# Splitting the last expert tiles, moving the weight maximum, filling idle TensorE time and finer loads ahead of the combination

## What is computed

```
h = layernorm(x) * (1 + ca) + sa
x = x + ga * linear_attention(h)      # 16 heads of 8, running sums over the tokens
h = layernorm(x) * (1 + cb) + sb
h = rmsnorm(h @ W_in.T, in_norm_w)    # then a router picks 2 of 8 experts per token
out = sum over the two: gate_e * rmsnorm((silu(h @ Wg[e].T) * (h @ Wu[e].T)) @ Wd[e].T, enorm_w[e])
x = x + gb * (rmsnorm(out, out_norm_w) @ W_out.T)
```

## Time and profile before

| | |
|---|---|
| median of the timed runs | 414.87 us |
| time of the profiled execution | 414.08 us |
| its span, first to last instruction | 412.2 us |
| PE busy | 354.4 us (86%) |
| DVE busy | 323.8 us (79%) |
| ACT busy | 291.9 us (71%) |
| POOL busy | 236.5 us (57%) |
| mean granted TensorE clock | 0.939 |

### The profile page before, as it was taken

How to read it: one execution, slowest core, us unless ns; L and a number is a source line. 1 busy time by engine, 2 the same in 40 slices (tenths; PEclk the granted TensorE clock), 3 DMA queues, 4 the chain that set the end, 5 groups by cost and what they waited for, 6 DMA issues and landing times.

```text
span 412.2 us, 12923 instructions
## 1 busy us (share of the span) xinstructions
PE 354.4 (86%) x3757; PEld 307.9 (75%) x3758; DVE 323.8 (79%) x1037; ACT 291.9 (71%) x814; POOL 236.5 (57%) x211
## 2 busy tenths in 40 slices
PE   7899998999999999982069999999999999990464
PEld 4788886888888888861049889989899898980443
DVE  5568998899999999976928887878778877870696
ACT  5465776888888888546328878778778787773595
POOL 0665585688888888856341645454454445453441
PEclk9999998999999999995559999999999999997698
DMA  7899000000000000111423333333333333213833
GB/s 217 356 368 363 2 28 26 8 30 27 26 26 26 26 26 26 34 40 51 131 40 54 68 71 70 62 71 60 64 64 71 60 69 65 57 34 110 351 94 94
DMA packets 46563, 35.68 MB, mean 87 GB/s; under 512 B 36291, under 2 KB 42070, under 8 KB 45750
## 3 DMA queue, kind: packets, MB, share of 16 engines
q1 hardware_dynamic: 41862, 25.40, 21.9%
q0 software_dynamic: 4544, 9.39, 7.0%
q10 hardware_dynamic: 128, 0.53, 0.5%
HBM read 18.69 MB, written 13.47 MB: 78 GB/s over the span
## 4 chain that ended last, share of the span: by engine, by line
PE 70%; DVE 10%; ACT 6%; issue 5%; DMA 4%; POOL 1%; SPq 1%; DVEq 0%; ACTq 0%; POOLq 0%
PE bank L1474 12%; PE bank L1723 9%; PE bank L1724 8%; PE bank L1725 8%; PE bank L1738 4%; PE bank L1740 4%; PE bank L1554 4%; PE bank L1739 4%; PE bank L1497 3%; DVE prod L960 2%; ACT junk L835 2%; DVE wmaxs L1056 1%; PE bank L1561 1%; DMA cst<-consts 1%; PE bank L1581 1%
## 5 line engine op out<-in xcount | busy, mean ns | idle before, releaser
L559 POOL DMA_INDIRECT expert_rows<-late,to_place x78 | 79.2, 1015 | 85.9 <-DVE late L1333 73.3
L1723 PE MATMUL bank<-late,w_hi 128*128 128x256 f16 x312 | 86.4, 277 | 15.1 <-DMA late<-dispatched 13.7
L1724 PE MATMUL bank<-late,w_hi 128*128 128x256 f16 x312 | 86.4, 277 | 0.0
L1725 PE MATMUL bank<-late,w_lo 128*128 128x256 f16 x312 | 86.3, 276 | 0.0
L518 POOL TENSOR_TENSOR kv<-kv,v 128x1024 f32<-128x1024 f32 x32 | 67.7, 2134 | 32.0 <-ACT kv L686 32.0
L1319 DVE SCALAR_TENSOR_TENSOR kv<-bank,uscale,kv 128x512 f32<-128x512 f32 x78 | 58.5, 750 | 30.4 <-ACT kv L777 18.6
L536 POOL DMA_INDIRECT dispatched<-rows,pos x64 | 67.3, 1051 | 25.7 <-issue 18.2
L1474 PE MATMUL bank<-cst,kv 128*128 128x128 f32 x576 | 74.3, 279 | 0.0
L777 ACT ACTIVATE kv<-bank,descale 128x512 f32<-128x512 f32 x78 | 53.6, 687 | 24.0 <-PE bank L1725 20.1
L1474 PEld LDWEIGHTS bank<-cst,kv 128*128 128x128 f32 x576 | 68.9, 193 | 0.3 <-issue 0.2
L783 ACT ACTIVATE kv<-kv 128x512 f16<-128x512 f32 x78 | 48.8, 625 | 16.8 <-DVE kv L1319 12.3
(11 more groups left out here) (233 smaller groups left out, 733.2 us busy)
## 6 DMA issues: line engine op xcount, KB each, us to landing
late<-wguT SPq DMA_DIRECT2D x1, 4096.0 KB, 17.8
late<-expert_rows SPq DMA_DIRECT2D x1, 2064.0 KB, 10.9
gates_bc<-gate_rows SPq DMA_DIRECT2D x1, 2048.0 KB, 6.9
wd<-wdT SPq DMA_DIRECT2D x1, 2048.0 KB, 25.0
out<-kv SPq DMA_DIRECT2D x16, 128.0 KB, 1.8
late<-dispatched SPq DMA_TRANSPOSE x78
expert_rows<-late,to_place POOLq DMA_INDIRECT x78
late<-expert_rows SPq DMA_DIRECT2D x1, 1032.0 KB, 6.5
```

The costliest lines, as they stand in the source:

```text
L559: pool.indirect_dma_start(ybuf, bass.IndirectOffsetOnAxis(ap=to_place[:, s, r:r + 1], axis=0), yt[:, s, r, :], None).then_inc(y_scat[s], 16)
L1723: mm(o, w_hi[:, w], hi, start=True, stop=False)
L1724: mm(o, w_hi[:, w], lo, start=False, stop=False)
L1725: last = mm(o, w_lo[:, w], hi, start=False, stop=True)
```

## The change

- **Maximum of the weights.** The first matmul goes in front of chunk 1 of half 1, `weight_power` after VectorE's products of half 1, the second matmul after `head_sums` at the end of the step (new semaphore `wall_ps`), `weight_scale` after `count_chosen`.
- **Filling matmuls.** `keep_busy(bank, n)` issues n matmuls of 128 x 128 by 512 columns in bf16 into a bank that nobody reads: 5, 13, 3 and 12 in the drain, 36 after `TOTAL`, 3 after the scatters have landed and 46 ahead of the combination.
- **Loads of tiles.** One transposing DMA of 256 columns in place of two of 128, and SyncE's waits for scatters and filler move behind the table and the register load.
- **Addresses of the weights** are taken in bytes (`columns_of`).
- **Last two tiles.** Squares, weighing and scatter go by 128 rows, the two blocks of a tile in different banks; the last `down` makes block 0 of a half before block 1.
- **Combination.** `LOADS` has five parts, (0, 1), (1, 2), (2, 4), (4, 8), (8, B); the square roots and coefficients of the second load come before the first batch, the others stand one place further on.

```diff
-        LOADS = [(0, 1), (1, 4), (4, 8), (8, B)]
+        LOADS = [(0, 1), (1, 2), (2, 4), (4, 8), (8, B)]
...
+        def last_rows_of(s, r):
+            return bk[s - LAST + 2][:, 0:D] if r else Y[s % 2][:, 0:D]
...
# SyncE
-            sp.wait_ge(scattered[0], 16 * NT * K * (B // 2))
-            sp.wait_ge(scattered[1], 16 * NT * K * (B // 2))
-            sp.wait_ge(filled, 16 * (E + 1))
             sp.wait_ge(table_done, 1)
...
-                for half in range(2):
-                    sp.dma_start(hT3[:, s, half], hbuf16[bass.ds(row, R), half * D:(half + 1) * D],
-                                 transpose=True).then_inc(slot_ld[s], 16)
+                sp.dma_start(hT3[:, s], hbuf16[bass.ds(row, R), 0:2 * D], transpose=True).then_inc(slot_ld[s], 16)
...
                 sp.load(row_regs, tile_row[0:1, bass.ds(TURN * i, TURN)])
+                if not again_turn(i):
+                    sp.wait_ge(filled, 16 * (E + 1))
+                    sp.wait_ge(scattered[0], 16 * NT * K * (B // 2))
+                    sp.wait_ge(scattered[1], 16 * NT * K * (B // 2))
...
# GpSimd
-            for s in range(LAST):
+            for s in range(LAST - 2):
                 scatter_tile(s, TURNS)
+            for s in range(LAST - 2, LAST):
+                for r in range(RB):
+                    pool.wait_ge(last_rows, RB * (s - LAST + 2) + r + 1)
+                    pool.indirect_dma_start(
...
# ScalarE
+            act.wait_ge(y_ps, TILES - 1)
+            last_square(LAST - 2, 0)
             high_part(TILES - 1, LAST - 1, TURNS - 1, 1)
-            for s in range(LAST - 2, LAST):
-                for r in range(RB):
-                    square(TILES - LAST + s, s, TURNS - 1, r)
+            last_square(LAST - 2, 1)
+            for r in range(RB):
+                act.wait_ge(last_y_ps, r + 1)
+                last_square(LAST - 1, r)
...
-                if isinstance(b, int) and b == 0:
-                    rms_of_rows(1)
...
             rms_of_rows(0)
+            rms_of_rows(1)
             for b in range(8):
                 norm_out(*batch_of_turn(0, b))
-                if b in (1, 5):
-                    rms_of_rows((1, 5).index(b) + 2)
+                if b in (0, 2, 5):
+                    rms_of_rows((0, 2, 5).index(b) + 2)
...
# VectorE
-                    if scale:
-                        weight_power(att)
...
                 if att is not None:
+                    running_products(att, 1)
                     if scale:
-                        weight_scale(att)
-                    running_products(att, 1)
+                        weight_power(att)
...
+                if scale:
+                    weight_scale()
...
+            weigh_row(LAST - 2, 0, dve.snap(last_ex[0], min_val=0, max_val=E - 1))
             low_part(TILES - 1, LAST - 1, TURNS - 1, 1)
-            for n in range(2):
-                weigh(TILES - 2 + n, LAST - 2 + n, TURNS - 1, dve.snap(last_ex[n], min_val=0, max_val=E - 1))
+            weigh_row(LAST - 2, 1, dve.snap(last_ex[0], min_val=0, max_val=E - 1))
+            for r in range(RB):
+                weigh_row(LAST - 1, r, dve.snap(last_ex[1], min_val=0, max_val=E - 1))
...
             coefficients(0)
+            coefficients(1)
             mix_experts(*batch_of_turn(0, 0))
-            coefficients(1)
             mix_experts(*batch_of_turn(0, 1))
+            coefficients(2)
...
# TensorE
-                    if scale and cc == 1:
-                        if t == 0:
-                            pe.wait_ge(wmax_done, 1)
-                            mm(MAX_ROW, wmax[:], ident, start=True, stop=True)
-                        else:
-                            pe.wait_ge(wpow_done, 1)
-                            mm(MAX_ALL, ones[0:1, :], wpow_row[:], start=True, stop=True)
+                    if scale and t and cc == 1:
+                        pe.wait_ge(wmax_done, 1)
+                        mm(MAX_ROW, wmax[:], ident, start=True, stop=True)
...
+                if scale:
+                    pe.wait_ge(wpow_done, 1)
+                    pe.wait_ge(ohs_done, rte[0] + 1)
+                    mm(MAX_ALL, ones[0:1, :], wpow_row[:], start=True, stop=True).then_inc(wall_ps, 1)
+
+            def keep_busy(bank, n):
+                for _ in range(n):
+                    mm(bank[:].rearrange("p (a n) -> p a n", n=P), ones16[:],
+                       ones16[:].unsqueeze(1).to_broadcast([P, 4, P]), start=True, stop=True)
...
                 head_sums(b15, 1)
+                pe.wait_ge(cum_used[1][1], B)
+                keep_busy(CUM[1], 5)
                 spread(*b15)
                 ranks(*b13)
                 turn(*b14)
                 project(*b15)
                 into_experts(*b14)
+                keep_busy(CUM[1], 13)
                 ranks(*b14)
                 turn(*b15)
+                keep_busy(CUM[1], 3)
                 into_experts(*b15)
+                keep_busy(CUM[1], 12)
                 ranks(*b15)
...
             mm(TOTAL, ones16[:], oh_all[:, B, NT * K, :], start=True, stop=True).then_inc(total_ps, 1)
+            keep_busy(CUM[0], 36)
...
+            def columns_of(w, e, per_expert, at):
+                return w.bitcast(U8)[:, bass.ds(e * (2 * per_expert) + 2 * at, 2 * P)].bitcast(F16)
...
+            def last_down(t, s, i, e):
...
+                pe.wait_ge(gulo_done, 2 * t + 1)
+                for r in range(RB):
+                    for f in range(FC // 2):
+                        part(r, f)
+                pe.wait_ge(gulo_done, 2 * t + 2)
+                for r in range(RB):
+                    for f in range(FC // 2, FC):
+                        last = part(r, f)
+                    last.then_inc(last_y_ps, 1)
...
+            pe.wait_ge(scattered[0], 16 * NT * K * (B // 2))
+            pe.wait_ge(scattered[1], 16 * NT * K * (B // 2))
+            keep_busy(CUM[0], 3)
             turn_of_tiles(0, first=True)
...
             pe.wait_ge(wgb_done, 1)
+            pe.wait_ge(last_rows, 2)
+            keep_busy(CUM[0], 46)
```

More of the change, by code:

```diff
@@ L21 @@
 U32 = mybir.dt.uint32
+U8 = mybir.dt.uint8
 ALU = mybir.AluOpType
@@ L315, in block_kernel @@
         ln_st, ln2_st = two("ln_st"), sem("ln2_st")
-        scattered, yb_ld, stored = two("scattered"), [sem(f"yb_ld{i}") for i in range(4)], four("stored")
+        scattered, yb_ld, stored = two("scattered"), [sem(f"yb_ld{i}") for i in range(5)], four("stored")
         lr_done, score_done, max_done, idx_done, oh_done = (
@@ L812, in _, with last_square @@
             turn_of_tiles(TURNS - 1, tiles=LAST)
+            def last_square(s, r):
+                act.wait_ge(ysq_done, RB * (TILES - LAST + s) + r)
+                nc.scalar.activation(junk3[:], last_rows_of(s, r), ACT.Square, scale=ydesc[:],
+                                     accum_out=yt[:, s, r, D:YW]).then_inc(ysq_done, 1)
+            act.wait_ge(y_ps, TILES - 1)
+            last_square(LAST - 2, 0)
             high_part(TILES - 1, LAST - 1, TURNS - 1, 1)
-            for s in range(LAST - 2, LAST):
-                for r in range(RB):
-                    square(TILES - LAST + s, s, TURNS - 1, r)
+            last_square(LAST - 2, 1)
+            for r in range(RB):
+                act.wait_ge(last_y_ps, r + 1)
+                last_square(LAST - 1, r)
             act.wait_ge(gate_diff, 1)
@@ L1415, in _ @@
             turn_of_batches(0, (2,))
-            coefficients(2)
+            coefficients(3)
             turn_of_batches(0, (3,))
             turn_of_batches(1, (0, 1, 2))
-            coefficients(3)
+            coefficients(4)
             turn_of_batches(1, (3,))
@@ L1720, in gate_up, with down @@
                     o = (G, U)[part][h][:, c * R:(c + 1) * R]
-                    w = bass.ds(e * F + (part * E * F + (h * (FC // 2) + c) * P), P)
-                    mm(o, w_hi[:, w], hi, start=True, stop=False)
-                    mm(o, w_hi[:, w], lo, start=False, stop=False)
-                    last = mm(o, w_lo[:, w], hi, start=False, stop=True)
+                    wh, wl = (columns_of(w[:], e, F, part * E * F + (h * (FC // 2) + c) * P) for w in (w_hi, w_lo))
+                    mm(o, wh, hi, start=True, stop=False)
+                    mm(o, wh, lo, start=False, stop=False)
+                    last = mm(o, wl, hi, start=False, stop=True)
                 last.then_inc((g_ps, u3_ps)[part], 1)
-            def down(t, s, i, e):
+            def down(t, s, i, e, apart=False):
                 if s >= 2 or again_turn(i):
@@ L1734, in down, with part @@
                         pe.wait_ge(gulo_done, 2 * t + h + 1)
-                    w = bass.ds(e * (FC * D) + f * D, D)
+                    wh, wl = (columns_of(w, e, FC * D, f * D) for w in (wd_hi, wd_lo))
                     for r in range(RB):
                         o, g = Y[s % 2][:, r * D:(r + 1) * D], slice(c * R + r * P, c * R + (r + 1) * P)
-                        mm(o, gu_hi[:, s % 2, h, g], wd_hi[:, w], start=(f == 0 and r == 0), stop=False)
```

(26 more changed lines are left out.)

21 lines of the change are left out of this document (15 added, 6 removed).

## The result

| | before | after |
|---|---|---|
| median of the timed runs | 415.15 us (20 runs, 413.69 to 416.89) | 412.68 us (20 runs, 410.00 to 414.63) |
| ratio | | 0.9933, 95% interval 0.9915 to 0.9952 |
| profiled execution, span | 414.08, 412.2 us | 413.16, 411.3 us |
| mean granted clock | 0.939 | 0.973 |

Faster by 2.5 us, where 8 were forecast (406.0, range 402 to 412). The clock's slices show where fills worked: the two fives of the drain are gone, but lows stand near 20, 75, 210 and 390 us.

What follows compares the result with a forecast made beforehand. TensorE was taken to bound the steps and experts, with losses at low-clock seams paced by chains through other engines. Seven terms summed to 8.05 us, so 414.08 would become 406.0 us, range 403.5 to 409, wider 402 to 412.

Steps and rivals of the forecast that it cites:

- turn of the maxima: Step 7: moving the weights' maximum shortens TensorE's 1.85 us idle time; 1.6 us won, bounds 0.3 and 3.5.
- drain: After the last step: fills hold the clock, so chain matmuls last 1.55 us instead of 3.3; 1.75 us won.
- first tile: Before the first expert tile: register load behind the scatters' landing 0.4, one wide transpose 0.7; 1.1 us won.
- clock at tile 0: First 27 expert matmuls at half clock lose 2.8 us; fills may hold it; 1.7 us won, bounds 0 and 2.8.
- addresses: Expert tiles: fewer register operations before each matmul cut idle time at turns' ends; 0.6 us won, bounds 0 and 1.9.
- last two tiles: End of expert stage: GpSimd's last four scatters start sooner by 128-row blocks; 0.5 us won, bounds -0.3 and 0.5.
- combination: Final stage: batch 1 gets its own load and starts sooner; 0.8 us won, bounds -0.3 and 1.5.
- if the clock holds: Step 7: with the clock up, L1554 comes at about 69.8 for 71.87, 2.1 us sooner; otherwise about 0.5 won.
- wait once each for their coefficients: Combination: batches 2 and 3 wait so, with batch 4 still at about 389.9 for 391.19.
- Rival C: Expert tiles: the wide transpose makes SyncE the bound, 17 us at 4.0 us each; 423 us, chance 0.05.
- A: Rival: clock falls in step 7, drain and at first tile; sum 1.4 us, so 412.7 us; chance 0.15.
- D: Rival: fills hide and cost nothing; first load, last tiles and combination pay about 2.4, 411.7 us; chance 0.09.

Runs made afterwards that it cites:

- e8: Changed kernel with a tile's rows loaded as two transposes of 128 columns instead of one of 256; ratio to before 0.9962.
- e9: Changed kernel with the weights' columns addressed in f16 elements as before, instead of bytes; ratio to before 0.9944.
- e2: Changed kernel with 42 fills in place of 36 and 12 in place of 3 ahead of tile 0; ratio to before 0.9873.
- e3: Changed kernel with the turn of the weights' maximum put back where it stood before; 422.79 us, ratio to before 0.9919.
- b_before: The kernel before, unchanged, measured once more on a chip with waits for remote; 430.69 us.
- e10: Changed kernel with the edits of e2 and e7 together; 421.73 us, ratio to before 0.9779.
- e11: e10 with the turn of the weights' maximum put back as in e3; ratio to before 0.9817.
- e13: e12 without the groups of 5, 13, 3 and 12 fills in the drain; 412.29 us, ratio to before 0.9935.
- e7: Changed kernel with the third group's root mean square computed ahead of norm_out(2) instead of behind it; 422.74 us, ratio to before 0.9830.
- e12: e10 again, on a chip like the first pair's; 409.29 us, ratio to before 0.9846.
- e16: e10 a third time, on a chip like the first pair's; 409.08 us, ratio to before 0.9878.
- Both repairs: Changed kernel with 42 and 12 fills ahead of tile 0 and the third root mean square one batch earlier (e10, e12, e16); ratios 0.9779, 0.9846, 0.9878.
- e14: e12 without the 46 fills ahead of the combination; 409.78 us, ratio to before 0.9869.
- e15: e10 with four fills ahead of the running state's last third and one behind it in step 7; 409.87 us, ratio to before 0.9872.

## Why the prediction was wrong in size

The signs of the whole and of most steps were right; four terms of the sum fail.

| term | forecast | shown |
|---|---|---|
| turn of the maxima | 1.6 | -0.34 in the profiled pair; +1.35 where the clock holds |
| drain | 1.75 | 1.15 against before; the fills alone 1.74 |
| first tile | 1.1 | 1.55, 0.35 of it a sooner landing of the scatters; 1.15 by e8 |
| clock at tile 0 | 1.7 | 0 in the profiled pair, 1.2 in e9; 2.9 with 15 more fills |
| addresses | 0.6 | 0 |
| last two tiles | 0.5 | 0.85 |
| combination | 0.8 | -0.83; -1.2 to +0.45 with one square root moved |
| sum | 8.05 | 2.4 |

- **Turn of the maxima.** The step on TensorE came out as written (1.04 us of wait for my 0.85). What failed is "if the clock holds": it fell in eight of 14 profiles, the first pair's among them. I priced the fall at 0.5 won; it costs 1.64 us. With the clock up in both kernels, the late turn is worth 0.5 us (25.07 in e2 and e8, 25.57 and 25.60 in e3 and b_before, on chips with waits for remote). With falls in about half of the executions that nets to some tenths, and e10 and e11 cannot be told apart.
- **Drain.** Mechanism and 1.74 us are right. Against before only 1.15 came, because before waited 1.20 at the first of the two groups, not the 1.77 of e13; in e13 the clock had fallen 17.4 us into the drain, for 19.5 before. GpSimd did become the bound in the end, at the place that the earlier trace rows allows.
- **Clock at tile 0**, the step that failed outright. The prediction set 3 us of idle time at 0.50 or 1.00 open and took the middle, 1.7. The gaps were 1.40 and 2.15 us, with 0.8 us of work between them, and the clock fell, for 6.8 us where it had been low for 5.5 us of the stretch before; in e9 it was 3.4. The argument for holding was the earlier trace rows, the 5 us after the experts; it does not carry over.
- **Addresses.** The waits at the turns' ends, from which I took 0.6, are 1.3 us in seven before and 1.2 in seven after, and e9 shows no other gain.
- **Combination.** I wrote that batches 2 and 3 "wait once each for their coefficients" and did not price it. It is 1.5 us by batch 4 (e7), since the square root stands behind `norm_out(2)` on ScalarE. The clock behind batch 4, on which the prediction has no word, adds up to 0.47 us at batch 7 and 0.56 at batches 9 to 12. The first load landed 2.68 us after its issue, as in the earlier trace rows; the second, issued 0.40 later, landed 2.94 after its own, inside my bounds (in e12 and e16 it took 3.9 and 4.0, which is outside). The Trainium skill, "DMA: Bandwidth & Descriptors", "Anatomy of one DMA", would have 2.6 by a fit for DMAs that GpSimd issues, while SyncE issues these; it does not move the sum.
- **First tile.** The wide transpose costs SyncE what one of the narrow ones did: three of them 3.96 us and single ones 1.20, where the earlier trace rows has 1.21 for half the columns, and lands 2.78 us after issue, where the second narrow one took 2.28. From the first issue to the rows that is 2.78 us for 3.64: 0.86 won for my 0.7. The register load gave 0.33 for my 0.4. Rival C falls with it.
- **Rivals.** A named 412.7, the median to 0.02 us, but by other terms: it had the drain lose 1.9, which it won, and the combination win 0.6, which it lost. Its place, step 7 and tile 0, was right. D's sum was near by chance too: fills in the drain do count.

## What to carry to other kernels

Fill a wait of TensorE to its end: two gaps of 1.4 and 2.2 us around three fills lost the clock, 15 more matmuls won 1.7 to 2.9 us, and 54 that started at the lower clock ended too late by themselves. When a load is cut finer, follow every consumer's queue to where the next piece's coefficients are made; the wait of 1.7 us had moved by two batches. Both repairs together took 0.985 and 0.988 of the kernel before on chips like the first, 0.978 on the others, against 0.993 and 0.988 for the change alone; e14 and e15, 0.987 each, cannot be told from them.

## What was unexpected of the hardware

- The same kernel takes 415 us or 427 to 432 us by the chip, and the traces of the slower ones have idle time marked "remote", on ScalarE and VectorE, mostly 1 to 3.9 us each, in the step after the turn of the maxima, in the drain and in the tiles' turns. What ends these waits no record shows. The Trainium skill, "Runtime: NRT & Kernel Launch", "Instruction fetch mechanics", has engines stream their instructions by DMA, mostly hidden, and stall at a branch whose target is not at hand. Whether these waits are such fetches no run here shows.
- On such chips, halving the number of transposing DMAs took 7.2 to 7.8 us off a stage whose rows were never late behind tile 0. ScalarE's remote waits are 8.9 us in both profiles with two transposes a tile (b_before, e8) and at most 4.5 with one; that e8 differs from the changed kernel by nothing else makes the transposes the cause. By which path they act is open.
- A transposing DMA of 256 columns costs SyncE 1.20 us, the same as one of 128.
- Whether the clock falls between 70 and 78 us differs from execution to execution of one kernel, at 1.64 us each (e12, e13, e16).
